# First stage: probabilities of tile pairs without zeros, weighting last, GpSimd's sum early; the mask's products in row halves

## The chip, the cores and the metric

The program runs on one core of a Trainium2 chip. The metric is the device time of one execution in microseconds (us), the smaller the better.

## The reference, cut to what matters

The program computes six residual layers over x of shape (32, 64, 256). Two of them matter here. The first is a causal attention with 16 heads of 128 over sequences of 64:

```
def _L0_attn_ref(x, W_Q, W_K, W_V, W_O, b_Q, b_K, b_V, b_O):
    q = jnp.einsum('bpd,hde->bphe', x, W_Q) + b_Q
    k = jnp.einsum('bpd,hde->bphe', x, W_K) + b_K
    v = jnp.einsum('bpd,hde->bphe', x, W_V) + b_V
    scores = jnp.einsum('bqhe,bkhe->bhqk', q, k) / ATTN_SCALE
    scores = jnp.where(causal, scores, IGNORE)
    attn = jax.nn.softmax(scores, axis=-1)
    z = jnp.einsum('bkhe,bhqk->bqhe', v, attn)
    out = jnp.einsum('bqhe,hed->bqd', z, W_O) + b_O
...
x = x + _L0_attn_ref(_layernorm(x, axis=-1), ...)
```

The others that the change touches are two causal attentions with 16 heads of 16 (one inside the third layer, one the fifth layer), whose scores get an additive mask:

```
scores = jnp.einsum('bgnqd,bgkd->bgnqk', qg, k) * scale
scores = jnp.where(causal, scores, jnp.asarray(-1e+30, scores.dtype))
attn = jax.nn.softmax(scores, axis=-1)
```

## The kernel before, in words

The 2048 tokens are 16 tiles of 128 partitions, and each tile holds two sequences of 64 tokens. x stays in on-chip memory (`x_rows`) through all stages. Products that need full accuracy are made of three products of high and low parts (`PARTS`).

**First stage** (`stage_L0_attention`). The normalised tokens are turned once (`split_tokens`) into `xnT`, with the model dimension on partitions. Then come 64 units, u = 4 x head + group of four tiles. One unit is, on TensorE (PE):

- `project` (L557): q and k of 512 tokens, six products of 512 columns each. For the even head of each pair of heads `values` (L539) makes the values of both heads, twelve products of 256 columns ahead of q and twelve behind k. So of every eight units four have values and four have none.
- `scores` (L572): eight products of 64 x 64, one for each sequence; fp32, so that each is two instructions in the trace.
- `turn` (L580): four transposes of the probabilities, 128 x 128 each. The probabilities of a tile's two sequences stand in `prob` as two 64 x 64 blocks on the diagonal of a 128 x 128 block whose other half is zeros.
- `weigh` (L589): z of each tile is one product of the turned block, 128 rows deep and 128 columns wide.
- `output` (L598): z times W_O, twelve products of 256 columns.

VectorE (DVE) does, for one unit: `shift` (L687 mask, L691 maximum, L693 subtraction), `normalise` (L717 sum, L719 reciprocal, L723 two products of 64 partitions each into `prob`), `z_low_part` (L682) and `add_out` (L701, x plus the result). ScalarE (ACT) does `q_copy` (L623), `k_copy` (L636), `v_copy` (L644), `probT_copy` (L632), `exponent` (L628) and `z_high_part` (L653), and `split_high` (L615, L618), the high parts of the next weights, once in four units.

Beside this the stage decodes the packed weights of the last layer (`Dequantiser`), one piece in four units, in phases: DVE `code` and `sign` (L2473, L2475), then `signed` (L2479), `sized` (L2484), `full` (L2490), one phase behind each unit; ACT two `over` (L2501, L2503) and later one half (L2508); GpSimd (POOL) the sum of the two `over` (`gpsimd_sum`, L2514), for which DVE's `sized` waits, and the low half (`gpsimd_low`, L2520). POOL also makes the low parts of the first stage's weights (`split_low`, L665, and L669 for the values).

The order on each engine is written out by hand: `run_steps` goes through a list of (part, lag) in every step s and gives part its unit s - lag. Each engine executes its own list in order, and semaphores tie the lists together. A part with a larger lag works on an older unit.

**The two masked attentions** (stages with tags s3a and s5a) go over 16 tiles each. Their scores are sums in PSUM: first the mask, as a product of the identity with the mask (L1283, `ident_r` 128 x 128 with `mask_r` 128 x 64 four times over, four such products of 256 columns for a tile), then the 32-row products of q and k on top of it (L1290).

## Time and profile before

| | us |
|---|---|
| median of 3 runs | 1754.83 |
| range of the runs | 1753.07 to 1756.31 |
| the profiled execution | 1752.43 |
| its span, first to last instruction | 1750.6 |

Busy shares of the span: PE 91%, DVE 62%, ACT 49%, POOL 38%. The mean granted clock of TensorE is 0.971 of full speed. The first stage's units run from 33 us (first scores) to some 559 us. A busy share is an average over stages; what bounds a stage is read from the order of instructions in it. PE's matmuls are pipelined: a group's busy time includes the tail of its last instruction, and what a group costs is read from its start to the start of the next.

### The profile page before, as it was taken

What the parts mean: (1) busy time and instruction counts of PE and PEld (TensorE: products, weight loads), DVE (VectorE), ACT (ScalarE), POOL (GpSimd) and SP (SyncE); (2) the same over time, 40 slices, a digit from 0 to 9 for tenths busy, and PEclk for the clock granted to TensorE, in tenths of its full rate; (3) what the DMA queues carried; (4) which work ended last, traced back from release to release, by engine and by line L of the source; (5) the groups of instructions that cost most, each with busy time, mean ns of one, the idle gap of its engine ahead of it and who ended that gap; (6) DMA issues with size and microseconds to landing.
All of it is one profiled execution on the core that took longest, in us unless ns stands there. A gap on an engine that the chain in (4) does not pass through costs nothing. (4 is left out here: it accounts for less than half of the span.)

```text
span 1750.6 us, 37012 instructions
## 1 busy us (share of the span) xinstructions
PE 1584.9 (91%) x14664; PEld 1281.7 (73%) x14664; DVE 1089.3 (62%) x1734; ACT 863.5 (49%) x1466; POOL 672.5 (38%) x527
## 2 busy tenths in 40 slices
PE   6999999999996887899999797899997898999998
PEld 4888888888885565777788564566664675888887
DVE  5777677677776888566442568999994565112111
ACT  3555555555453565555422346667672674222222
POOL 0111211211212663531422265999994430232332
PEclk9999999999998999899999799999998898999999
DMA  3011111111112300010102120000000900000000
GB/s 105 16 64 55 40 63 60 33 63 60 37 59 78 109 2 26 8 12 10 40 1 105 28 64 1 1 2 1 2 1 26 360 17 1 1 13 12 1 12 12
DMA packets 72351, 70.26 MB, mean 40 GB/s; under 512 B 24816, under 2 KB 64368, under 8 KB 71840
## 3 DMA queue, kind: packets, MB, share of 16 engines
q1 hardware_dynamic: 72224, 68.46, 12.2%
q8 instruction: 93, 1.52, 0.4%
q14 instruction: 34, 0.28, 0.1%
HBM read 46.03 MB, written 19.27 MB: 37 GB/s over the span
## 5 line engine op out<-in xcount | busy, mean ns | idle before, releaser
L665 POOL TENSOR_TENSOR s_w_parts<-s_w_raw,s_w_parts 128x768 fp32r<-128x768 f32 x15 | 27.8, 1855 | 401.9 <-ACT s_w_parts L615 401.9
L1488 DVE TENSOR_TENSOR s6f_hid<-s6f_act_sb,s6f_u_ps 128x512 f32<-128x512 f32 x64 | 44.0, 688 | 218.4 <-PE s6f_u_ps L1439 218.4
L1511 POOL TENSOR_TENSOR s6f_hid_parts<-s6f_hid,s6f_hid_parts 128x512 fp32r<-128x512 f32 x64 | 82.7, 1291 | 224.3 <-ACT s6f_hid_parts L1477 224.3
L2228 POOL TENSOR_TENSOR s4b_with_q<-s4b_with_q 128x1024 f32<-128x1024 f32 x64 | 150.8, 2378 | 0.4 <-DVE s4b_with_q L2183 0.4
L2183 DVE TENSOR_TENSOR s4b_with_q<-s4b_c_ps,s_q_rows 128x2048 f32<-128x2048 f32 x64 | 146.1, 2285 | 1.2 <-PE s4b_c_ps L2322 1.1
L598 PE MATMUL s_o_ps<-s_w_parts,s_zT 128*128 128x256 f32 x768 | 110.6, 294 | 4.1 <-DVE x_rows L701 4.1
L539 PE MATMUL s_v_ps<-s_wv_parts,s_xnT 128*128 128x256 f32 x768 | 104.6, 286 | 8.2 <-ACT s_v L644 6.8
L1477 ACT ACTIVATE s6f_hid_parts<-s6f_hid 128x512 fp32r<-128x512 f32 x64 | 40.5, 632 | 144.5 <-PE s6f_o_ps L1459 141.0
L539 PEld LDWEIGHTS s_v_ps<-s_wv_parts,s_xnT 128*128 128x128 f32 x768 | 97.0, 191 | 13.8 <-ACT s_v L644 10.0
L1459 PEld LDWEIGHTS s6f_o_ps<-s6w_parts,s6f_hid_parts 128*128 128x128 f32 x768 | 99.2, 188 | 6.8 <-issue 1.0
L598 PEld LDWEIGHTS s_o_ps<-s_w_parts,s_zT 128*128 128x128 f32 x768 | 97.3, 193 | 8.8 <-issue 4.5
L1439 PE MATMUL s6f_g_ps<-s_zT,s6w_parts 128*128 128x512 f32 (+1 forms) x384 | 101.2, 398 | 1.2 <-PEq L283 1.2
L557 PE MATMUL s_q_ps<-s_xnT,s_w_parts 128*128 128x512 f32 x384 | 101.7, 400 | 0.0
L1459 PE MATMUL s6f_o_ps<-s6w_parts,s6f_hid_parts 128*128 128x256 f32 x768 | 100.7, 280 | 0.8 <-POOL s6f_hid_parts L1511 0.8
L1439 PE MATMUL s6f_u_ps<-s_zT,s6w_parts 128*128 128x512 f32 (+1 forms) x384 | 100.5, 396 | 0.0
L628 ACT ACTIVATE s_ex<-s_sc 128x256 f32<-128x256 f32 x64 | 26.7, 417 | 149.2 <-DVE s_sc L693 149.2
L557 PE MATMUL s_k_ps<-s_xnT,s_w_parts 128*128 128x512 f32 x384 | 98.5, 392 | 0.0
L2306 PE MATMUL s4b_turns_ps<-s_theta_parts,s_z_parts 128*128 128x512 f32 x192 | 62.8, 435 | 26.3 <-DVE s4b_frac L2166 24.5
L1439 PEld LDWEIGHTS s6f_u_ps<-s_zT,s6w_parts 128*128 128x128 f32 x384 | 72.3, 188 | 18.0
L557 PEld LDWEIGHTS s_k_ps<-s_xnT,s_w_parts 128*128 128x128 f32 x384 | 72.1, 188 | 15.8
L1511 POOL TENSOR_TENSOR s3f_hid_parts<-s3f_hid,s3f_hid_parts 128x512 fp32r<-128x512 f32 x32 | 42.3, 1321 | 104.7 <-ACT s3f_hid_parts L1477 104.7
L701 DVE TENSOR_TENSOR x_rows<-x_rows,s_o_ps 128x1024 f32<-128x1024 f32 x64 | 77.5, 1210 | 1.6 <-PE s_o_ps L598 1.6
(333 smaller groups left out, 3982.0 us busy)
## 6 DMA issues: line engine op xcount, KB each, us to landing
stored_weights<-s1q_halves SPq DMA_DIRECT2D x16, 768.0 KB, 3.7
s6w_parts<-stored_weights SPq DMA_DIRECT2D x32, 384.0 KB, 7.6
s1q_packed<-in_codes SPq DMA_DIRECT2D x8, 384.0 KB, 4.4
s1q_scale<-in_scale_rows SPq DMA_DIRECT2D x8, 384.0 KB, 4.9
s3p_raw<-in_ffn_pieces SPq DMA_DIRECT2D x8, 384.0 KB, 8.5
early_values<-s_vbd SPq DMA_DIRECT2D x1, 2176.0 KB, 12.3
s_vbd<-early_values SPq DMA_DIRECT2D x4, 544.0 KB, 7.0
x_rows<-in_x SPq DMA_DIRECT2D x4, 512.0 KB, 5.4
```

The source lines that it names most:

```text
L539: last = nc.tensor.matmul(v_ps[:, n * 2 * E:(n + 1) * 2 * E], xnT[:, px, c, g * TG + t, :], wv_parts[:, pw, c, :, :], start=(c == 0 and (p ...
L557: last = nc.tensor.matmul(ps[:, :], weights(slot, pw, m, c), xnT[:, px, c, g * TG:(g + 1) * TG, :], start=(c == 0 and (pw, px) == PARTS[0] ...
L598: last = nc.tensor.matmul(o_ps[:, t // 2, (t % 2) * D:(t % 2 + 1) * D], zT[:, pz, t * P:(t + 1) * P], w_parts[:, k // G, pw, 2, :], start= ...
L701: nc.vector.tensor_tensor(core.x[:, t0:t0 + TG, :], core.x[:, t0:t0 + TG, :], o_ps[:, :, :].rearrange("p b (t n) -> p (b t) n", t=2), ALU. ...
L1439: last = nc.tensor.matmul(ps[:, s, :], wt(pw, c, f), zT[:, pz, c:c + 1, bass.ds(rnd * TG, TG), :] .rearrange("p c t q -> p (c t) q"), star ...
L1459: last = nc.tensor.matmul(o_ps[:, t, 0:D], hid_parts[:, f % 2, ph, t * P:(t + 1) * P], down_w(pw, f), start=(f == 0 and (ph, pw) == PARTS[0]),
L1477: nc.scalar.activation(hid_parts[:, f % 2, 0, :], hid[:, f % 2, :], ACT.Copy).then_inc(high_done, 1)
L1488: nc.vector.tensor_tensor(hid[:, f % 2, :], act_sb[:, f % 2, :], u_ps[:, f % 2, :], ALU.mult) \
L1511: nc.gpsimd.tensor_tensor(hid_parts[:, f % 2, 1, :], hid[:, f % 2, :], hid_parts[:, f % 2, 0, :], ALU.subtract).then_inc(low_done, 1)
L2183: nc.vector.tensor_tensor(with_q[:, half, :, :, :, :, :].rearrange("p (a n) q j s c -> p n a q (j s) c", n=2) [:, n_, :, :, :, :], src.uns ...
L2228: nc.gpsimd.tensor_tensor(with_q[:, half, :, 0, :, n_, :], with_q[:, half, :, 0, :, n_, :], with_q[:, half, :, 1, :, 1 - n_, :], op).then_ ...
L2306: last = nc.tensor.matmul(turns_ps[:, :], z_parts[:, pz, half, bass.ds(i * P, P)], theta_parts[:, pt, half, n_ * 512:(n_ + 1) * 512], star ...
```

## The change

**Tokens in pairs.** `split_tokens` gets `pairs=True` in the first stage: `xnT` holds two tiles 2i and 2i+1 as (first sequences of both, second sequences of both). So the 128 tokens of one `values` product are sequence b of both tiles of a pair, and the products of q and k run over the same tokens in this order.

**Probabilities without zeros.** `prob` is [P, 2, TG, S] (two buffers), written by one product over 128 partitions in place of two over 64. `turn` is two transposes for a unit in place of four: one transposes the blocks of two tiles side by side. The turned block then holds tile n's keys in rows n x 64 and queries of both sequences in its columns. `weigh` takes eight products in place of four, each 64 rows deep, 128 columns of weights, 64 columns moving, and those of n = 0 and n = 1 lie in the two halves of the rows and write to two banks of `z_ps`. `probT_copy` copies 256 columns in place of 512. `z_ps` takes two banks; to make room, `s_ps` and `pT_ps` share one bank, and with it come two waits: `scores` of u also waits for `pT_out` of u - 1 copies, and `turn` of u for `masked` up to u + 2.

**Order in the step.** PE: from project, turn, scores, output, weigh to project, turn, output, scores, weigh, with turn and weigh one unit older (lag 5) and output too (lag 6). ACT: `z_high_part` before `exponent`. DVE: `add_out` first, `z_low_part` before `normalise`. POOL: from split_low, sum, low to low, sum, split_low. The zeroing of `prob` goes.

**The mask's products.** `ident_r` holds in each half of its rows the 64 x 64 identity twice side by side, and product j reads only the row half j % 2: 64 rows deep, 256 columns as before.

```
-            prob = room.sb("prob", [P, TG, P])
-            probT = room.sb("probT", [P, TG * P])
-            zT = room.sb("zT", [P, 2, TG * P], F32R)
+            prob = room.sb("prob", [P, 2, TG, S])
+            probT = room.sb("probT", [P, TG * S])
+            zT = room.sb("zT", [P, 2, 2, 2 * P], F32R)
...
+            sp_ps = room.ps("sp_ps", [P, 512])
+            s_ps, pT_ps = sp_ps[:, 0:TG * S], sp_ps[:, TG * S:2 * TG * S]
+            z_ps = room.ps("z_ps", [P, 2, 512])
...
                     wait(pe, masked, u)
+                    wait(pe, pT_out, u - 1)
...
-                    for t in range(TG):
-                        last = nc.tensor.transpose(pT_ps[:, t * P:(t + 1) * P], prob[:, t, :], core.c("ident"))
+
+                    pe.wait_ge(masked, min(u + 2, U) if isinstance(u, int) else u + 2)
+                    for pair in range(2):
+                        last = nc.tensor.transpose(pT_ps[:, pair * P:(pair + 1) * P],
+                                                   prob[:, k % 2, 2 * pair:2 * pair + 2, :].rearrange("p t s -> p (t s)"),
+                                                   core.c("ident"))
...
-                    for t in range(TG):
-                        last = nc.tensor.matmul(z_ps[:, t * P:(t + 1) * P], v[:, k % G, t, k // G, :],
-                                                probT[:, t * P:(t + 1) * P], start=True, stop=True)
+                    for pair in range(2):
+                        for b in range(2):
+                            for n in range(2):
+                                rows, at = slice(n * S, (n + 1) * S), pair * P + b * S
+                                last = nc.tensor.matmul(z_ps[:, n, at:at + S], v[rows, k % G, pair, b, k // G, :],
+                                                        probT[rows, at:at + S], start=True, stop=True)
...
-                run_steps(pe, U, [(project, 3), (turn, 4), (scores, 3), (output, 5), (weigh, 4)], unroll=8)
+                run_steps(pe, U, [(project, 3), (turn, 5), (output, 6), (scores, 3), (weigh, 5)], unroll=8)
...
-                run_steps(act, U, [(v_copy(0), 3), (q_copy, 3), (k_copy, 3), (v_copy(1), 3), (probT_copy, 4), (exponent, 3),
-                                   (z_high_part, 4), (split_high, 0), (deq.scalar, 4)], unroll=8)
+                run_steps(act, U, [(v_copy(0), 3), (q_copy, 3), (k_copy, 3), (v_copy(1), 3), (probT_copy, 5),
+                                   (z_high_part, 5), (exponent, 3), (split_high, 0), (deq.scalar, 4)], unroll=8)
...
-                run_steps(pool, H, [(split_low, 0), (lambda j, rnd, slot: deq.gpsimd_sum(j), 1),
-                                    (lambda j, rnd, slot: deq.gpsimd_low(j, slot), 2)])
+                run_steps(pool, H, [(lambda j, rnd, slot: deq.gpsimd_low(j, slot), 2),
+                                    (lambda j, rnd, slot: deq.gpsimd_sum(j), 1), (split_low, 0)])
...
-                nc.vector.memset(prob[:, :, :], 0.0).then_inc(zeroed, 1)
-                dve.wait_ge(zeroed, 1)
...
-                    for b in range(2):
-                        rows = slice(b * S, (b + 1) * S)
-                        last = nc.vector.tensor_tensor(prob[rows, :, b * S:(b + 1) * S], ex[rows, :, :],
-                                                       rs[rows, :].unsqueeze(2).to_broadcast([S, TG, S]), ALU.mult)
-                    last.then_inc(prob_done, 1)
-
-                run_steps(dve, U, [(shift, 3), (normalise, 3), (z_low_part, 4), (add_out, 5), (deq.vector, 3)],
+                    wait(dve, pT_full, u - 1)
+                    nc.vector.tensor_tensor(prob[:, k % 2, :, :], ex[:, :, :],
+                                            rs[:, :].unsqueeze(2).to_broadcast([P, TG, S]), ALU.mult) \
+                        .then_inc(prob_done, 1)
+
+                run_steps(dve, U, [(add_out, 6), (shift, 3), (z_low_part, 5), (normalise, 3), (deq.vector, 3)],
                           unroll=8)
...
-                    nc.tensor.matmul(s_ps[:, j, 0:4 * S].rearrange("p (h s) -> p h s", s=S), ident_r[:, :],
-                                     mask_r[:, :].unsqueeze(1).to_broadcast([P, 4, S]), start=True, stop=False)
+                    half = slice(j % 2 * S, (j % 2 + 1) * S)
+                    nc.tensor.matmul(s_ps[:, j, 0:4 * S].rearrange("p (h s) -> p h s", s=S), ident_r[half, :],
+                                     mask_r[half, :].unsqueeze(1).to_broadcast([S, 4, S]), start=True, stop=False)
```

The order on PE before, in a step of a unit with values (L580 turn, L572 scores, L598 output, L589 weigh, L539 values, L557 q and k):

```order
L580 MATMUL s_pT_ps<-const,s_prob 128x128 x4
L572 MATMUL s_s_ps<-s_kT,s_qT 64x64 x8
L598 MATMUL s_o_ps<-s_w_parts,s_zT 128x256 x12
L589 MATMUL s_z_ps<-s_probT,s_v 128x128 x4
L539 MATMUL s_v_ps<-s_wv_parts,s_xnT 128x256 x12
L557 MATMUL s_q_ps<-s_xnT,s_w_parts 128x512 x6
L557 MATMUL s_k_ps<-s_xnT,s_w_parts 128x512 x6
L539 MATMUL s_v_ps<-s_wv_parts,s_xnT 128x256 x12
```

The same place on PE in the changed kernel (L589 is now turn, L612 output, L579 scores, L603 weigh):

```order
L589 MATMUL s_sp_ps<-const,s_prob 128x128 x2
L612 MATMUL s_o_ps<-s_w_parts,s_zT 128x256 x12
L579 MATMUL s_sp_ps<-s_kT,s_qT 64x64 x8
L603 MATMUL s_z_ps<-s_probT,s_v 128x64 x8
L543 MATMUL s_v_ps<-s_wv_parts,s_xnT 128x256 x12
L562 MATMUL s_q_ps<-s_xnT,s_w_parts 128x512 x6
L562 MATMUL s_k_ps<-s_xnT,s_w_parts 128x512 x6
L543 MATMUL s_v_ps<-s_wv_parts,s_xnT 128x256 x12
```

Between the last k product and the scores stood four transposes; now two transposes and the twelve output products stand there, and the scores and the weighting follow each other.

DVE before, one step of the first stage, from the mask of one unit to the decoding's phase behind it:

```order
L687 TENSOR_TENSOR s_sc<-s_s_ps,const 128x256
L691 TENSOR_REDUCE s_mx<-s_sc 128x4
L693 TENSOR_TENSOR s_sc<-s_sc,s_mx 128x256
L717 TENSOR_REDUCE s_sm<-s_ex 128x4
L719 RECIPROCAL s_rs<-s_sm 128x4
L723 TENSOR_TENSOR s_prob<-s_ex,s_rs 64x4x64 x2
L682 SCALAR_TENSOR_TENSOR s_zT<-s_z_ps,s_bias,s_zT 128x512
L701 TENSOR_TENSOR x_rows<-x_rows,s_o_ps 128x1024
L2484 TENSOR_TENSOR s1q_sized<-s1q_over,s1q_code 128x768
```

The same step on DVE in the changed kernel, with what each instruction waits for:

```order
L712 TENSOR_TENSOR x_rows<-x_rows,s_o_ps 128x1024 [waits s1_o_full]
L698 TENSOR_TENSOR s_sc<-s_sp_ps,const 128x256 [waits s1_s_full]
L702 TENSOR_REDUCE s_mx<-s_sc 128x4 [waits s1_masked]
L704 TENSOR_TENSOR s_sc<-s_sc,s_mx 128x256 [waits s1_maxed]
L693 SCALAR_TENSOR_TENSOR s_zT<-s_z_ps,s_bias,s_zT 128x512 [waits s1_z_high]
L728 TENSOR_REDUCE s_sm<-s_ex 128x4 [waits s1_exped]
L730 RECIPROCAL s_rs<-s_sm 128x4 [waits s1_summed]
L733 TENSOR_TENSOR s_prob<-s_ex,s_rs 128x256 [waits s1_pT_full,s1_inverted]
L2505 SCALAR_TENSOR_TENSOR s1q_full<-s1q_sized,s1q_signed 128x768 [waits s1q_low_done,s1q_scaled,s1q_sized_done]
```

The addition to x (L712) now stands ahead of the mask, z's low part inside the wait for the exponential, and one product of 128 partitions is left of two.

POOL before, in its loop (L665 and L669 low parts of the stage's weights, L2514 sum, L2520 low half of the decoded piece):

```order
L665 TENSOR_TENSOR s_w_parts<-s_w_raw,s_w_parts 128x768
L669 TENSOR_TENSOR s_wv_parts<-s_wv_raw,s_wv_parts 128x512
L2514 TENSOR_TENSOR s1q_over<-s1q_over 128x768
L2520 TENSOR_TENSOR s1q_halves<-s1q_full,s1q_halves 128x768
L665 TENSOR_TENSOR s_w_parts<-s_w_raw,s_w_parts 128x768
```

POOL in the changed kernel (L2535 low half, L2529 sum, L679 and L683 weights):

```order
L2535 TENSOR_TENSOR s1q_halves<-s1q_full,s1q_halves 128x768
L2529 TENSOR_TENSOR s1q_over<-s1q_over 128x768
L679 TENSOR_TENSOR s_w_parts<-s_w_raw,s_w_parts 128x768
L683 TENSOR_TENSOR s_wv_parts<-s_wv_raw,s_wv_parts 128x512
L2535 TENSOR_TENSOR s1q_halves<-s1q_full,s1q_halves 128x768
```

The sum no longer stands behind the weights of the next head, whose high parts ACT makes a step later.

## Rows read from the trace of the kernel before

**Rows 1.** First stage, 100 us: busy PE, PEld, DVE, ACT, POOL; granted clock; DMA
```profile
200.00:300.00 100.00, 95.18 (x782) 84.66 (x782) 72.36 (x127) 52.18 (x89) 18.79 (x11) 1.00 0.17 56
```

**Rows 2.** Waits of PE between 55 and 545 us: us in total, times, longest
```profile
PE s_s_ps L572 <- issue: 13.0, 31, 0.6
```

**Rows 3.** Timeline of PE: one unit without values (start us, us, instruction)
```profile
201.62 0.69 PE L572 MATMUL s_s_ps<-s_kT,s_qT 128*64 128x64 f32 x16 [0.39 <-issue]
202.23 1.69 PE L598 MATMUL s_o_ps<-s_w_parts,s_zT 128*128 128x256 f32 x12
203.76 1.05 PE L589 MATMUL s_z_ps<-s_probT,s_v 128*128 128x128 f32 x8
204.57 1.62 PE L557 MATMUL s_q_ps<-s_xnT,s_w_parts 128*128 128x512 f32 x6
206.03 1.54 PE L557 MATMUL s_k_ps<-s_xnT,s_w_parts 128*128 128x512 f32 x6
207.41 0.60 PE L580 MATMUL s_pT_ps<-const,s_prob 128*128 128x128 f32 x4
208.52 0.69 PE L572 MATMUL s_s_ps<-s_kT,s_qT 128*64 128x64 f32 x16 [0.52 <-issue]
```

**Rows 4.** Timeline of PE: units with values, the first of a round and the next
```profile
215.31 0.69 PE L572 MATMUL s_s_ps<-s_kT,s_qT 128*64 128x64 f32 x16 [0.39 <-issue]
...
223.57 1.65 PE L539 MATMUL s_v_ps<-s_wv_parts,s_xnT 128*128 128x256 f32 x12 [0.93 <-ACT s_v L644]
...
225.58 0.69 PE L572 MATMUL s_s_ps<-s_kT,s_qT 128*64 128x64 f32 x16
...
234.22 0.60 PE L580 MATMUL s_pT_ps<-const,s_prob 128*128 128x128 f32 x4
...
234.74 0.69 PE L572 MATMUL s_s_ps<-s_kT,s_qT 128*64 128x64 f32 x16
```

**Rows 5.** Timeline of ACT and DVE in the first of these units
```profile
218.17 2.58 DVE L2484 TENSOR_TENSOR s1q_sized<-s1q_over,s1q_code 128x768 f32<-128x768 f32 x1 [3.68 <-POOL s1q_over L2514]
...
222.93 0.59 ACT L644 ACTIVATE s_v<-s_v_ps 128x512 f32<-128x512 f32 x1
```

**Rows 6.** Timeline of ACT in the unit of rows 3
```profile
203.72 0.42 ACT L628 ACTIVATE s_ex<-s_sc 128x256 f32<-128x256 f32 x1 [1.71 <-DVE s_sc L693]
...
205.52 0.93 ACT L2501 ACTIVATE s1q_over<-s1q_code,const 128x768 f32<-128x768 int32 x1
...
207.17 0.67 ACT L623 ACTIVATE s_qT<-s_q_ps,s_bias 128x512 f32<-128x512 f32 x1
207.74 0.68 ACT L636 ACTIVATE s_kT<-s_k_ps,s_bias 128x512 f32<-128x512 f32 x1
```

**Rows 7.** Eight matmuls of row halves, late stage: ns min/median/max, first and last start
```profile
L2345 PE MATMUL s4b_y_ps<-s_w_bd,s4b_outT x8: 482/482/587, 1170.0 to 1171.1; 64*128 64x384 f32 x8
```

**Rows 8.** Groups of DVE between 100 and 500 us (busy us, mean ns)
```profile
L701 DVE TENSOR_TENSOR x_rows<-x_rows,s_o_ps 128x1024 f32<-128x1024 f32 x50 | 60.5, 1210 | 0.0
...
L723 DVE TENSOR_TENSOR s_prob<-s_ex,s_rs 64x256 f32<-64x256 f32 x100 | 42.0, 420 | 2.4
```

**Rows 9.** Single lines of DVE over the run: ns min/median/max, starts
```profile
L2484 DVE TENSOR_TENSOR s1q_sized<-s1q_over,s1q_code x16: 945/2566/2584, 57.6 to 542.3; 128x768 f32<-128x768 f32 x16
...
L693 DVE TENSOR_TENSOR s_sc<-s_sc,s_mx x64: 424/425/1150, 35.1 to 544.1; 128x256 f32<-128x256 f32 x64
...
L2479 DVE SCALAR_TENSOR_TENSOR s1q_signed<-s1q_sign,s1q_scale x16: 950/952/2400, 45.1 to 532.7; 128x768 f32<-128x768 int32 x16
```

**Rows 10.** Timeline of PE: the mask's products in stage s5a
```profile
1388.91 0.74 PE L1283 MATMUL s5a_s_ps<-s5a_mask_r,s5a_ident_r 128*128 128x256 f32 x4
1389.58 0.69 PE L1290 MATMUL s5a_s_ps<-s5a_kbd,s5a_qT 32*64 32x128 f32 x32
```

**Rows 11.** Waits of PE between 1370 and 1445 us (s5a)
```profile
PE s5a_va_ps L1337 <- DVE x_rows L1112: 0.6, 4, 0.2
```

**Rows 12.** Waits of POOL between 100 and 500 us
```profile
POOL s_w_parts L665 <- ACT s_w_parts L615: 316.9, 12, 28.7
```

More of the change, by code:

```diff
@@ L272, with split_tokens @@
 PARTS = ((0, 0), (0, 1), (1, 0))
-def split_tokens(core, parts, mv, factor, tag, column_step=1, beside=None, high_beside=None):
+def split_tokens(core, parts, mv, factor, tag, column_step=1, beside=None, high_beside=None, pairs=False):
     nc = core.nc
@@ L290, in rows, with place @@
         def rows(t):
+            if pairs:
+                return turned[:, t % 4, 0:D].rearrange("p (c b s) -> p c b s", c=NC, b=2)
             return turned[:, t % 4, 0:D].rearrange("p (c q) -> p c q", c=NC)
+        def place(part, t):
+            return parts[:, part, :, t // 2, :, t % 2, :] if pairs else parts[:, part, :, t, :]
         @block.vector
@@ L296, in low @@
                 dve.wait_ge(high_done, t + 1)
-                nc.vector.tensor_tensor(parts[:, 1, :, t, :], rows(t), parts[:, 0, :, t, :], ALU.subtract) \
+                nc.vector.tensor_tensor(place(1, t), rows(t), place(0, t), ALU.subtract) \
                     .then_inc(low_done, 1)
@@ L319, in _ @@
                 act.wait_ge(turned_done, t + 1)
-                nc.scalar.activation(parts[:, 0, :, t, :], rows(t), ACT.Copy).then_inc(high_done, 1)
+                nc.scalar.activation(place(0, t), rows(t), ACT.Copy).then_inc(high_done, 1)
                 if high_beside and t in (3, 9):
@@ L414, in stage_L0_attention @@
         oroom = Room(nc, octx, "s1")
-        xnT = oroom.sb("xnT", [P, 2, NC, NT, P], F32R)
+        xnT = oroom.sb("xnT", [P, 2, NC, NT // 2, 2, 2, S], F32R)
         mv = oroom.sb("mv", [P, NT, 2])
@@ L481, in low_weights @@
                                     ALU.subtract).then_inc(wv_low, 1)
-        split_tokens(core, xnT, mv, rstd, "s1t", beside=low_weights, high_beside=high_weights)
+        split_tokens(core, xnT, mv, rstd, "s1t", pairs=True, beside=low_weights, high_beside=high_weights)
         with ExitStack() as ctx:
@@ L487, in stage_L0_attention @@
             kT = room.sb("kT", [P, TG * P])
-            v = room.sb("v", [P, G, TG, 2, E])
+            v = room.sb("v", [P, G, 2, 2, 2, E])
             sc = room.sb("sc", [P, TG, S])
@@ L499, in stage_L0_attention @@
             v_ps = room.ps("v_ps", [P, 512])
-            s_ps = room.ps("s_ps", [P, 512])
-            pT_ps = room.ps("pT_ps", [P, 512])
-            z_ps = room.ps("z_ps", [P, 512])
+            sp_ps = room.ps("sp_ps", [P, 512])
+            s_ps, pT_ps = sp_ps[:, 0:TG * S], sp_ps[:, TG * S:2 * TG * S]
+            z_ps = room.ps("z_ps", [P, 2, 512])
             o_ps = room.ps("o_ps", [P, 2, 512])
             (q_full, k_full, v_full, s_full, pT_full, z_full, q_out, k_out, v_out,
-             masked, maxed, shifted, exped, summed, inverted, prob_done, pT_out, z_high, z_low, o_out, zeroed) = room.sems(
+             masked, maxed, shifted, exped, summed, inverted, prob_done, pT_out, z_high, z_low, o_out) = room.sems(
                 "q_full", "k_full", "v_full", "s_full", "pT_full", "z_full",
                 "q_out", "k_out", "v_out", "masked", "maxed", "shifted", "exped", "summed", "inverted",
-                "prob_done", "pT_out", "z_high", "z_low", "o_out", "zeroed")
+                "prob_done", "pT_out", "z_high", "z_low", "o_out")
             block = ctx.enter_context(nc.Block())
@@ L535, in values @@
                     for n in range(2):
-                        t = 2 * half + n
                         for c in range(NC):
@@ L539, in values @@
                                 last = nc.tensor.matmul(v_ps[:, n * 2 * E:(n + 1) * 2 * E],
-                                                        xnT[:, px, c, g * TG + t, :], wv_parts[:, pw, c, :, :],
+                                                        xnT[:, px, c, g * 2 + half, n, :, :].rearrange("p t s -> p (t s)"),
+                                                        wv_parts[:, pw, c, :, :],
                                                         start=(c == 0 and (px, pw) == PARTS[0]),
@@ L643, in part @@
                         act.wait_ge(v_full, u + k + half + 1)
-                        nc.scalar.activation(v[:, k, 2 * half:2 * half + 2, :, :],
-                                             v_ps[:, :].rearrange("p (t h e) -> p t h e", t=2, h=2), ACT.Copy) \
+                        nc.scalar.activation(v[:, k, half, :, :, :],
+                                             v_ps[:, :].rearrange("p (b h e) -> p b h e", b=2, h=2), ACT.Copy) \
                             .then_inc(v_out, 1)
@@ L1060, in _ @@
         def _(dve):
-            nc.vector.tensor_copy(ident_r[:, :], core.c("ident")).then_inc(masks, 1)
+            for b in range(2):
+                rows = slice(b * S, (b + 1) * S)
+                last = nc.vector.tensor_copy(ident_r[rows, :].rearrange("p (a s) -> p a s", a=2),
+                                             core.c("ident")[rows, rows].unsqueeze(1).to_broadcast([S, 2, S]))
+            last.then_inc(masks, 1)
             nc.vector.tensor_copy(mask_r[:, :], core.c("mask_add")).then_inc(masks, 1)
```

13 lines of the change are left out of this document (7 added, 6 removed).

## The prediction

> **What bounds the kernel now.** I read the views in this order: busy time by stretches, PE's waits, PE's timeline, then the timelines of the engines that PE waits for. In the first stage PE is busy 95 of 100 us at the full clock, DVE 72, ACT 52, POOL 19 [rows 1]. So PE sets the end there, and what I must count is the time from the start of one unit's scores to the start of the next. PE's waits are few by the list: the longest is 13 us in all, in front of the scores [rows 2].
>
> A unit without values takes 208.52 - 201.62 = 6.90 us [rows 3]. From start to start: scores 0.61, output 1.53, weigh 0.81, q 1.46, k 1.38, turn to scores 1.11. In the last of these the reader is to see the hidden wait: four transposes fill some 0.45 us, and the rest, about 0.65 us, is PE waiting for k's copy, which starts at 207.74 and takes 0.68 [rows 6], so it is over 0.1 us before the scores start.
>
> A unit with values takes 234.74 - 225.58 = 9.16 us; there turn to scores is only 0.52 us [rows 4], since the second half of values covers k's copy. The first such unit of each round of eight takes 225.58 - 215.31 = 10.27 us [rows 4]. Its extra 1.1 us comes in front of the second half of values, which waits for ACT's v copy at 222.93 [rows 4, 5]; and ACT is late because DVE sat idle 3.68 us for POOL's sum and then spent 2.58 us on `sized` [rows 5]. A round of eight is thus 10.27 + 3 x 9.16 + 4 x 6.8 = 65.0 us (most of the units without values take 6.8, the unit of rows 3, which has the two `over` on ACT, 6.9). There are eight rounds.
>
> **The change part by part.**
>
> *Turn.* Two transposes fewer. Four take about 0.45 us, so 0.22 us goes from each unit.
>
> *k's copy.* Output, 1.53 us, now stands between k and the scores. Turn (0.22) and output together are 1.75 us against the 1.11 us from k's end to the scores in which the copy was waited for. The copy of the turned probabilities, which the scores now also wait for, comes right behind k's copy. It has 256 columns, as the exponential has, which takes 0.42 us [rows 6]: by 1.11 + 0.4 = 1.5 us it is done, 0.25 us before PE is there. The 0.65 us of waiting goes in the four units without values; in the others nothing of it was there.
>
> *Weigh.* Eight matmuls, 16 instructions, in place of 8 instructions in 0.81 us. No row shows exactly this shape. The scores have 16 instructions of the same 64 columns, two in parallel in halves of the columns, and take 0.61 us [rows 3]. For halves of the rows there is L2345, 64 rows by 128 columns, 384 moving columns in fp32: its eight instructions start within 1.1 us [rows 7]. At the rate of weigh now (0.1 us for 128 columns) 384 columns are 0.3 us, and eight one behind another would start over 7 x 0.3 = 2.1 us. So they run two at a time. I take 0.61 us, as for the scores, which saves 0.2. The other bounds: 0.5 us if the half-deep weights come in faster; and 16 x 0.11 + 0.15 = 1.9 us if each instruction cost what one of 128 columns does now.
>
> *Change of tile form.* The four mask products of 256 columns between two other forms take 0.67 us [rows 10]; output's twelve of the same width take 1.53, 0.13 each [rows 3]. So about 0.15 to 0.2 us goes on two changes of form, and I charge 0.1 us for the one more that a unit has now (scores to weigh to q, before scores to output).
> The Trainium skill says in TensorEngine Tiling (Array Packing), Key Properties, that changing the tiling mode, not just the tile, drains TensorE. By that rule the third mode in each unit costs; without it the first stage would come out 64 x 0.1 = 6 us shorter. The trace agrees that something like 0.1 us is paid.
>
> The step of PE is then: without values 0.61 + 0.61 + 1.46 + 1.38 + 0.22 + 1.53 + 0.1 = 5.9 us; with values 9.16 - 0.22 - 0.2 + 0.1 = 8.85 us.
>
> *The chain through the scores.* What is late next when PE does not wait? The chain is scores, DVE's mask, maximum, subtraction, ACT's exponential, what ACT does behind it, q copy, k copy, probabilities' copy, next scores. From scores to the exponential it is 203.72 - 201.62 = 2.10 us [rows 6, 3]. Now `add_out`, 1.21 us [rows 8], stands ahead of the mask and starts about 0.25 us behind the scores' start, so the mask starts some 0.65 us later: 2.75. The exponential is 0.45. In one unit of four the two `over` follow, 207.17 - 205.52 = 1.65 us; then q copy 0.57 (207.17 to 207.74) [rows 6], and k copy, 0.57, and the probabilities' copy with its signal, 0.5. That is 6.5 us, over PE's 5.9. In another unit of four ACT makes high parts of weights, up to two copies of nearly the same size, and I charge the same 6.5. In the other two the chain is under 5.9. With values (8.85) it never decides. So 2 x 0.6 = 1.2 us a round.
>
> *POOL's order.* `sized` no longer waits 3.7 us. The 1.1 us in front of values goes once a round.
>
> *DVE.* It is busy 72.4% of a round of 65.0 us, 47.1 us [rows 1]; one of two products into `prob` goes, eight times 0.42 [rows 8]: 43.7 us, 5.5 a unit, under 5.9. This has little room, see the rivals. The waits for the shared bank (turn for `masked`, given a step earlier) are met more than 2 us ahead. The zeroing of `prob` is a single instruction at the stage's start, and the last units drain one step later, in which PE's work is hidden in the same chain: I take nothing for both, bounds -1 and +2 us.
>
> Round: 4 x 8.85 + 2 x 5.9 + 2 x 6.5 = 60.2 us against 65.0, 4.8 less; times eight is 38 us.
>
> *The mask's products.* Now 0.67 us for four of 256 columns [rows 10]; as two pairs that run at once I take two slots of 0.13 and the two changes of form, about 0.4 us: 0.27 us less, for 2 x 16 tiles. PE waits for next to nothing in that loop, 0.6 us in all for the worst [rows 11], so it carries: 32 x 0.27 = 8.6, and I take 8. Bounds: 0 if something else is next at once, 10 at best.
>
> Sum: 38 + 8 = 46 us. The profiled execution took 1752.43 us, 1.8 outside its span; less 46 it is 1706.4. The median of the runs is 2.4 us above it, and since the forecast is for a median I name 1708.
>
> **The rivals.**
>
> *PE decides throughout* (no chain, and weigh at 0.5). Speaks for it: the slack before and behind the chain may let late copies be caught up in the values units. Round 4 x 8.75 + 4 x 5.8 = 58.2, 6.8 less, 54 in all, with 9 for the masks: 1754.8 - 63 = 1692.
>
> *DVE becomes the bound, through POOL.* `sized` takes 945 ns at best and 2566 in the median, `signed` 952 and once 2400, the subtraction 425 and once 1150 [rows 9]: each has two tensors in on-chip memory, and in the long ones POOL was at work. Until now POOL waited once in four units, for the weights' high parts, 12 times in 400 us, and for nothing else that the list names [rows 12]: its instructions ran in one burst, part of it while DVE stood idle. Now they come in three different steps, each beside busy DVE work: `sized`, as before, `signed` (+1.45), and the product into `prob` twice a piece (up to +0.7 each by the subtraction's row, more if it comes early in POOL's instruction). That is +2.9 for four units, 5.9 a round: 49.6 us, 6.2 a unit. Over values units it is hidden, in the others it makes 6.6 to 7 of 5.9 or 6.5, since an instruction that is held makes `add_out` late and with it the chain. Round some 62.3, 2.7 less, 22 in all; with 8 of the masks 1725. Against it: most of the values units can absorb what piles up.
> The Trainium skill, GPSIMD Engine Reference, Specifications, says that GpSimd shares its SBUF interfaces with VectorE, with contention where VectorE has two SBUF inputs or a 2-port mode. The trace agrees for the two-input ones (2566 against 945 ns). By this rule `code` and `sign` could be held as well, for which no row here shows a case.
>
> *The masks give nothing* and the first stage what I say: 1716.
>
> *Slower than before: the row halves of weigh don't run together.* Its place is the group of 16 instructions behind the scores. If each costs what one of 128 columns costs now, weigh is 1.9 us, a unit without values 7.2, one with values 10.1, the round 69.2 us, 4.2 more; times eight 34, less 8: 1781. The point from which it decides: the round without weigh and without the chain is 4 x (8.24 + 5.3) = 54.2, so weigh must stay under (65.0 - 54.2 + 1) / 8 = 1.5 us (the 1 is the masks' share). Against it stands L2345's row, the same tile form.
>
> **How the numbers follow.** Chances: the forecast 0.5 (its own range 1698 to 1718), PE throughout 0.2, DVE with POOL 0.18, masks give nothing 0.08, slower 0.04. The two around the forecast on either side are taken in: the range is 1691 to 1731. A measurement of this kernel can tell about 0.2%, 3.5 us, from no change. Faster by more 0.94, within 0.02, slower 0.04.
>
> **What would show it.** In the profile after: scores to scores 5.9 us in units without values and about 8.85 in those with them; no unit of 10.3; weigh starting 0.61 us ahead of q; no idle time of DVE for POOL's sum; `prob` as one product of 0.42 us. If two units a round show 6.5, ACT or DVE in front of the scores is what I said. Long `prob` and `signed` instructions and a scores wait would show the DVE rival. In s3a and s5a the mask group should start 0.4 us ahead of the 32-row products. The forecast is wrong if weigh takes over 0.9 us, or if units without values average over 6.6 us.

## The result, and the profile after

The changed kernel takes 1734.4 us (median of 4 runs, 1731.17 to 1740.51) against 1754.62 for the kernel before (4 runs, 1753.07 to 1756.31): ratio 0.9889, 95% interval 0.9858 to 0.9919. It is faster, as forecast, but by 20 us where 46 were forecast, and the time lies outside the range of 1691 to 1731. The profiled executions differ by 1752.43 - 1731.17 = 21.3 us.

PE is busier than in [rows 1], at the same clock, and DVE less (busy by windows; the columns are those of [rows 1]):

```profile
200.00:300.00 100.00, 97.36 (x880) 87.01 (x879) 68.06 (x120) 53.35 (x93) 22.20 (x12) 1.00 0.17 56
```

The timeline of PE: first the groups of a unit without values, which answer to [rows 3], then the starts of the scores of later units, the first step without values (205.37 to 212.73), the next two with them:

```profile
190.76 0.38 PE L589 MATMUL s_sp_ps<-const,s_prob 128*128 128x128 f32 x2
190.90 1.67 PE L612 MATMUL s_o_ps<-s_w_parts,s_zT 128*128 128x256 f32 x12
192.50 0.69 PE L579 MATMUL s_sp_ps<-s_kT,s_qT 128*64 128x64 f32 x16
193.11 1.11 PE L603 MATMUL s_z_ps<-s_probT,s_v 64*128 64x64 f32 x16
194.15 1.67 PE L562 MATMUL s_q_ps<-s_xnT,s_w_parts 128*128 128x512 f32 x6
...
205.37 0.69 PE L579 MATMUL s_sp_ps<-s_kT,s_qT 128*64 128x64 f32 x16 [0.27 <-ACT s_probT L646]
...
212.73 0.69 PE L579 MATMUL s_sp_ps<-s_kT,s_qT 128*64 128x64 f32 x16 [1.01 <-ACT s_probT L646]
...
221.82 0.69 PE L579 MATMUL s_sp_ps<-s_kT,s_qT 128*64 128x64 f32 x16
...
230.83 0.69 PE L579 MATMUL s_sp_ps<-s_kT,s_qT 128*64 128x64 f32 x16
```

From start to start: turn 0.14 us, output 1.60, scores 0.61, weigh 194.15 - 193.11 = 1.04. The forecast had 0.61 for weigh, and before it was 0.81 [rows 3]. The units with values take 221.82 - 212.73 = 9.09 and 230.83 - 221.82 = 9.01 us, and that first one is no longer the 10.27 us of [rows 4]. The unit before it takes 212.73 - 205.37 = 7.36 us, with a wait of 1.01 us for ACT that was not in the forecast. Over the stage the starts of the scores are 6.27, 6.27, 6.61 and 7.2 to 8.05 us apart without values, 9.00 to 9.13 and once 9.74 with them. The six rounds of eight units in the middle of the stage take 62.4 to 63.3 us, 62.8 in the mean, against 65.0 before and 60.2 forecast.

The same unit on ACT; before, [rows 6] showed the overs and the copies without a break:

```profile
207.73 0.41 ACT L642 ACTIVATE s_ex<-s_sc 128x256 f32<-128x256 f32 x1
209.69 0.85 ACT L629 ACTIVATE s_w_parts<-s_w_raw 128x768 fp32r<-128x768 f32 x1 [1.56 <-DMA s_w_raw<-in_L_attn_W_O]
210.53 0.63 ACT L632 ACTIVATE s_wv_parts<-s_wv_raw 128x512 fp32r<-128x512 f32 x1
211.06 0.67 ACT L637 ACTIVATE s_qT<-s_q_ps,s_bias 128x512 f32<-128x512 f32 x1
211.63 0.68 ACT L650 ACTIVATE s_kT<-s_k_ps,s_bias 128x512 f32<-128x512 f32 x1
212.20 0.38 ACT L646 ACTIVATE s_probT<-s_sp_ps 128x256 f32<-128x256 f32 x1
```

ACT waits 1.56 us for the next head's weights before it makes their high part; q's, k's and the probabilities' copies are queued behind, and the scores wait for the last of them. SP's queue shows why the weights are late:

```profile
205.29 0.33 SPq L442 DMA_DIRECT2D s_bias<-in_bias_L  x1
205.89 0.38 SPq L446 DMA_DIRECT2D s_w_raw<-in_L_attn_W_Q  x1
206.37 0.42 SPq L446 DMA_DIRECT2D s_w_raw<-in_L_attn_W_K  x1
206.97 0.34 SPq L449 DMA_DIRECT2D s_w_raw<-in_L_attn_W_O  x1
```

The bias load, ahead of the weights, waits until the head two before has had its last output (its buffer is shared), and output now comes one step later.

On DVE nothing waits for POOL any more, and another instruction is held in place of `sized` (ns min/median/max of each line; [rows 9] has `sized` at 945/2566/2584 before, where `code` was 551/555/561):

```profile
L2488 DVE TENSOR_SCALAR s1q_code<-s1q_packed x16: 552/2200/2216, 38.2 to 510.0; 128x768 int32<-128x768 int32 x16
...
L2499 DVE TENSOR_TENSOR s1q_sized<-s1q_over,s1q_code x16: 943/951/953, 54.3 to 522.8; 128x768 f32<-128x768 f32 x16
```

The mask's products in stage s5a, against [rows 10]: the next group starts 0.43 us behind them instead of 0.67.

```profile
1370.58 0.50 PE L1298 MATMUL s5a_s_ps<-s5a_mask_r,s5a_ident_r 64*128 64x256 f32 x4
1371.01 0.69 PE L1305 MATMUL s5a_s_ps<-s5a_kbd,s5a_qT 32*64 32x128 f32 x32
```

The loops of s3a and s5a shrank from 103.70 to 98.58 us and from 83.19 to 79.95 us, 8.4 together. The rest came from the first stage. Its scores, first to last, took 506.97 us and take 490.37, 16.6 less. They begin 1.2 us later (34.59 us instead of 33.42), and from the last scores to the start of the last `add_out` it is 20.1 us instead of 17.8.

### The profile page after: what moved, and what is told of

Read it like the earlier page. It is cut to its first block and busy times, and to the rows that moved or that the text cites. A ratio compares the mean times of both kernels' runs of the same rounds, so it can differ in the third digit from the quotient of the medians.

```text
span 1729.4 us, 37862 instructions
## 1 busy us (share of the span) xinstructions
PE 1577.0 (91%) x15048; PEld 1270.1 (73%) x15048; DVE 1056.8 (61%) x1671; ACT 849.3 (49%) x1466; POOL 678.7 (39%) x527
## 3 DMA queue, kind: packets, MB, share of 16 engines
q8 instruction: 95, 1.56, 0.4%
## 5 line engine op out<-in xcount | busy, mean ns | idle before, releaser
L712 DVE TENSOR_TENSOR x_rows<-x_rows,s_o_ps 128x1024 f32<-128x1024 f32 x64 | 78.0, 1219 | 135.2 <-PE s_o_ps L612 135.2
L667 ACT ACTIVATE s_zT<-s_z_ps,s_bias 128x512 fp32r<-128x512 f32 x64 | 44.1, 689 | 150.0 <-PE s_z_ps L603 150.0
L612 PE MATMUL s_o_ps<-s_w_parts,s_zT 128*128 128x256 f32 x768 | 110.1, 294 | 4.6 <-DVE s_zT L693 4.6
L2535 POOL TENSOR_TENSOR s1q_halves<-s1q_full,s1q_halves 128x768 fp32r<-128x768 f32 x16 | 33.3, 2084 | 200.6 <-ACT s1q_halves L2523 200.6
L612 PEld LDWEIGHTS s_o_ps<-s_w_parts,s_zT 128*128 128x128 f32 x768 | 98.2, 194 | 5.6 <-DVE s_zT L693 5.6
```

The source lines that it names most:

```text
L612: last = nc.tensor.matmul(o_ps[:, t // 2, (t % 2) * D:(t % 2 + 1) * D], zT[:, pz, t % 2, t // 2 * P:(t // 2 + 1) * P], w_parts[:, k // G, ...
L667: nc.scalar.activation(zT[:, 0, :, :], z_ps[:, :, 0:2 * P], ACT.Identity, bias=bias[:, k // G, 2:3]) \
L712: nc.vector.tensor_tensor(core.x[:, t0:t0 + TG, :], core.x[:, t0:t0 + TG, :], o_ps[:, :, :].rearrange("p b (t n) -> p (b t) n", t=2), ALU. ...
```

## The experiments

"Before" in each ratio is the kernel before, run on the same chip. The median of each kernel and the ratio with its 95% interval:

| kernel | us | ratio to before |
|---|---|---|
| output ahead of scores, alone | 1784.28 | 1.0181 (1.0166 to 1.0195) |
| mask's row halves, alone | 1746.40 | 0.9965 (0.9952 to 0.9977) |
| GpSimd's order, alone | 1742.99 | 0.9942 (0.9929 to 0.9955) |
| all orders and halves, zeros kept | 1737.19 | 0.9912 (0.9897 to 0.9928) |
| the change | 1734.40 | 0.9889 (0.9858 to 0.9919) |
| zeros kept, loads early | 1730.18 | 0.9869 (0.9851 to 0.9887) |
| the change, loads early | 1728.25 | 0.9852 (0.9836 to 0.9869) |
| the change, weigh in quarters | 1717.42 | 0.9786 (0.9770 to 0.9802) |
| both | 1711.33 | 0.9762 (0.9745 to 0.9778) |
| both, decoder in ACT's gap | 1707.49 | 0.9745 (0.9730 to 0.9760) |
| the same, values' weights first | 1703.88 | 0.9726 (0.9709 to 0.9742) |

**Weigh in quarters.** Each product of 64 rows by 128 columns of weights becomes two of 64 by 64, behind a product of one column that carries the waits.

```
+ matmul(z_ps[0:64, 0, 256:257], v[:, ..., 0:64], probT[:, 0:1])
+ for half in range(2):  cols = slice(half * 64, half * 64 + 64)
-   matmul(z_ps[:, n, at:at+S],    v[rows, ..., :],    probT[rows, at:at+S])
+   matmul(z_ps[cols, n, at:at+S], v[rows, ..., cols], probT[rows, at:at+S])
```

> The changed kernel with weigh in quarters: the 128 columns of weights (v) are loaded as two halves of 64, so a unit has 16 products of 64 rows x 64 columns, four at a time in the quarters of the array, behind one product of one column that carries the wait. Theory A (the load of 128 columns of fp32 weights sets weigh's pace, 0.112 us for each pair, as 0.058 us goes with 64 columns in the scores): weigh takes about 0.75 us from its first product to q in place of 1.04, units without values that wait for nothing 5.95 to 6.0 in place of 6.27, with values 8.7 in place of 9.01; the units with a wait for ACT (6.6, 7.3) stay nearly as they are. About 2 us a round, 14 to 17 us in all: some 1718. Theory B (two products in row halves stream their columns one after the other, 2 x 0.056): weigh stays at 1.0 us or grows with the switch of form, and the time stays within 3 us of the changed kernel's.

Measured 1717.42 us (1715.21 to 1720.01), 17 less than the change. PE's timeline, one unit:

```profile
193.75 0.69 PE L579 MATMUL s_sp_ps<-s_kT,s_qT 128*64 128x64 f32 x16
194.27 0.23 PE L599 MATMUL s_z_ps<-s_probT,s_v 128*64 128x1 f32 x2
194.43 0.69 PE L607 MATMUL s_z_ps<-s_probT,s_v 64*64 64x64 f32 x32
195.05 1.65 PE L562 MATMUL s_q_ps<-s_xnT,s_w_parts 128*128 128x512 f32 x6
```

Thirty-two instructions take 0.62 us where sixteen took 1.04, for the same multiplications; with the product of one column, weigh is 0.78 us, and the scores ahead of it take 0.52 us instead of 0.61. Steps are 8.73 with values and 5.9 without; where ACT's chain or the late weights set the end, 6.6 to 6.96 and once 7.5.

**Half of the columns.** In the change, weigh streams 32 of each 64 columns of probabilities from the third unit on (the other half of z is not computed).

```
- probT[rows, at:at + S]
+ probT[rows, at:at + 32]
```

> The changed kernel with weigh moving only 32 of the 64 query columns of each product from the third unit on (half of z isn't computed anew). Theory A (weights' load sets the pace): the pairs of weigh still start 0.112 us apart and the group of 16 takes 1.04 us as before. Theory B (the streams of columns set it): pairs 0.06 us apart, the group about 0.6 us.

One run, 1742.71 us. The weigh group, in the timeline:

```profile
194.70 1.08 PE L604 MATMUL s_z_ps<-s_probT,s_v 64*128 64x32 f32 x16
195.71 1.66 PE L562 MATMUL s_q_ps<-s_xnT,s_w_parts 128*128 128x512 f32 x6
```

With half of the streaming it still takes 1.01 us, and its pairs still start 112 ns apart. So the moving columns don't set the pace of weigh. The weights' load is what is left, and the trace has records of it (PEld; ns min/median/max of one), here for weigh before, in the change and in quarters:

```profile
L589 PEld LDWEIGHTS s_z_ps<-s_probT,s_v x512: 186/192/331, 41.1 to 552.1; 128*128 128x128 f32 x171
...
L603 PEld LDWEIGHTS s_z_ps<-s_probT,s_v x1024: 182/188/334, 49.3 to 540.0; 64*128 64x128 f32 x171
...
L607 PEld LDWEIGHTS s_z_ps<-s_probT,s_v x2048: 129/135/223, 48.9 to 523.9; 64*64 64x64 f32 x187
```

Half of the rows leave a load as long as it was (188 ns against 192), half of the columns shorten it (135). The whole was not faster: four units with values take 10.55 to 10.59 us, each behind a unit with late weights, and the granted clock falls in them (0.54 between 152 and 154 us, in the first of them). One run doesn't tell whether that belongs to the edit.

**Weights loaded first.** The DMAs of the weights go ahead of SP's wait for the output, and the bias load, which alone needs it, behind them.

```
- wait(sp, o_full, ...);  dma(bias ...)
  wait(sp, w_low, h - 1)
  dma(w_raw ...) x3;  dma(wv_raw ...) x2
+ wait(sp, o_full, ...);  dma(bias ...)
```

> The changed kernel with one thing in the order of the loads: the DMAs of the next head's weights are issued ahead of SP's wait for the last output of the head before last, and only the bias load stays behind it. Theory: with output one step later that wait ends later, the weights land late, and ACT waits 1.6 us for them in one unit of four; in units without values this reaches the scores. Then ACT's wait for w_raw goes, that unit takes 6.3 to 6.6 in place of 7.2 to 8.0, and the time is 5 to 7 us less than the changed kernel's (about 1728), with less spread between runs. Rival: the loads are late for another reason (the DMA queue, the wait for the low parts): the unit stays at 7.3 and the time too.

Measured 1728.25 us (1724.38 to 1728.52); the profiled span is 1722.6 against 1729.4. In ACT's timeline the high parts now run on without a wait:

```profile
203.95 0.41 ACT L642 ACTIVATE s_ex<-s_sc 128x256 f32<-128x256 f32 x1
204.26 0.83 ACT L629 ACTIVATE s_w_parts<-s_w_raw 128x768 fp32r<-128x768 f32 x1
205.00 0.62 ACT L632 ACTIVATE s_wv_parts<-s_wv_raw 128x512 fp32r<-128x512 f32 x1
```

The units without values are 6.27, 6.27, 6.61 and 6.26 us in every round: the fourth was late only for its weights. The intervals of the two ratios overlap a little, so it is the profile that shows the gain: from the first scores to the last it is 481.6 us instead of 490.4.

**Both together.**

> Both edits at once. If they are independent, 20 to 23 us less than the changed kernel, about 1712. If ACT's chain (exponential, the two copies of the decoder or of the weights, q, k, probabilities) is next, units with this work stay at 6.4 to 6.6 and the sum is smaller, 1716.

Measured 1711.33 us (1710.79 to 1714.60). A round is 4 x 8.73 + 5.9 + 5.93 + 6.95 + 5.87 = 59.6 us; only the unit with the two overs is still set by ACT's chain.

**The mask alone**, in the kernel before:

> The kernel before with only the mask's products in row halves. Theory: 8 us less (1746 to 1747), since PE waits for next to nothing in the two loops: from the mask group's start to the 32-row products 0.4 us in place of 0.67, 0.27 us for each of 32 tiles. Rival: other waits of the loops take it up, and the time stays within 2 us of before.

Measured 1746.40 us; the two loops take 98.6 and 79.4 us in the profile, 8.9 less. The medians differ by 6.3 us (4.0 to 8.4 by the interval).

**GpSimd's order alone**, in the kernel before:

> The kernel before with only GpSimd's order changed (low half, sum, weights). Theory: the first unit with values of each round takes 9.1 to 9.2 us in place of 10.3, 1.1 us for eight rounds, 9 us in all: 1746. DVE's idle time for POOL's sum goes; code takes 2.2 us beside POOL and sized 0.95 in place of 2.57. Rival: what DVE is held beside POOL now comes on the path, and the time stays at 1752 to 1755.

Measured 1742.99 us, 9.7 less: the first unit with values takes 9.06 us in place of 10.28 (scores in PE's timeline):

```profile
214.93 0.69 PE L572 MATMUL s_s_ps<-s_kT,s_qT 128*64 128x64 f32 x16 [0.39 <-issue]
223.99 0.69 PE L572 MATMUL s_s_ps<-s_kT,s_qT 128*64 128x64 f32 x16
```

**Output ahead of scores alone**, in the kernel before, with no other list or lag changed:

```
- (turn, 4), (scores, 3), (output, 5), (weigh, 4)
+ (turn, 4), (output, 5), (scores, 3), (weigh, 4)
```

> The kernel before with only PE's order in the step changed: output ahead of the scores, with the lags of before and nothing else. Theory: k's copy is hidden by output, so units without values take 6.2 us in place of 6.8, with one of four held at some 6.6 by ACT's chain; 2.0 to 2.4 us a round, 16 to 19 us in all: 1736 to 1739. The units with values stay at 9.16. Rival: with output ahead of them the scores and all behind them on DVE and ACT come later, and what was waited for at the scores is waited for at turn or output: no more than 5 us.

Measured 1784.28 us, 32 us slower: neither the expected gain nor its rival came. The units without values take 7.7 us instead of 6.8. PE's waits name the cause:

```profile
PE s_o_ps L598 <- DVE x_rows L701: 38.3, 37, 1.3
```

Output waits for `add_out` of the unit before, which is last in DVE's list but for the decoder. The reordering is a loss unless `add_out` is first on DVE and everything behind turn is one lag later, as the change has it.

**The order alone.** The kernel before with all lists, lags, row halves and GpSimd's order of the change, but the probabilities with their zeros (in two buffers), four transposes, eight products in weigh and two products into `prob`.

```
- prob[P, TG, P]                     transpose(prob[:, t, :])
+ prob[P, 2, TG, P]                  transpose(prob[:, k % 2, t, :])
- PE  turn 4, scores 3, output 5, weigh 4
+ PE  turn 5, output 6, scores 3, weigh 5      (ACT and DVE as in the change)
```

> The kernel before with the change's order alone: its lists and lags on PE, ACT and DVE, GpSimd's order and the mask's row halves, while prob keeps its zeros (doubled, since it is written earlier than it is turned), with four transposes and the eight products of weigh as before. Theory: the probabilities without zeros brought PE nothing, because what two transposes less save (about 0.25 us) the slow weigh takes back (1.04 against 0.81 us) together with the third change of tile form. A unit without values is then 0.61 + 1.53 + 0.81 + 1.46 + 1.38 + 0.45 = 6.25 us, one with values 9.16; the time is that of the changed kernel within 0.5%, 1728 to 1742. Rival: the zero-free form was worth what was forecast for its turn and for DVE's one product (0.42 us a unit); then steps are 6.5 us or more everywhere and the time is 1748 or above. Second rival: DVE, with one product more, becomes the bound beside GpSimd: add_out no longer waits for output, and the steps are 6.6 to 6.9 with PE waiting for the output's or the scores' release.

Measured 1737.19 us (1734.14 to 1739.56). One unit of PE:

```profile
195.03 0.69 PE L572 MATMUL s_s_ps<-s_kT,s_qT 128*64 128x64 f32 x16
195.64 1.16 PE L589 MATMUL s_z_ps<-s_probT,s_v 128*128 128x128 f32 x8
196.56 1.63 PE L557 MATMUL s_q_ps<-s_xnT,s_w_parts 128*128 128x512 f32 x6
198.02 1.54 PE L557 MATMUL s_k_ps<-s_xnT,s_w_parts 128*128 128x512 f32 x6
199.41 0.60 PE L580 MATMUL s_pT_ps<-const,s_prob 128*128 128x128 f32 x4
199.76 1.67 PE L598 MATMUL s_o_ps<-s_w_parts,s_zT 128*128 128x256 f32 x12
201.36 0.69 PE L572 MATMUL s_s_ps<-s_kT,s_qT 128*64 128x64 f32 x16
```

Turn is 0.35 us instead of 0.14, weigh 0.92 instead of 1.04: a step of 6.33 us against 6.27 (0.45 and 0.81 were expected of turn and weigh; their sum is right). The theory holds, both rivals fall, though the units with values take 9.07 us where 9.16 were expected. Row halves and GpSimd's order alone give 0.9965 x 0.9942 = 0.9907, so with the weights late the new order of steps gives nothing on top; it does in the next kernel.

**The same with the loads first.**

> As the order-only kernel, with the weights' DMAs put ahead of the wait for the output. It is to be compared with the changed kernel with the same loads (1728.25). Theory: no unit of over 7 us for late weights; units without values 6.25 us (6.6 in the one with the two overs), with values 9.16: a round of 61.95 + 0.35 against 9.01 x 4 + 6.27 x 3 + 6.61 = 61.46, so 64/8 x 0.8 = 7 us longer at most, 1728 to 1737. Rival (the zero-free form has worth of its own): 1742 or more.

Measured 1730.18 us (1728.44 to 1731.07). Steps 9.07 and 6.33, 6.33, 6.85, 6.31. The two pairs with and without zeros differ by 0.2%, and their intervals overlap: what the zero-free form itself brought, in the shape it was given, is at most a few us. By the profiles of the pair with early loads it is 5.4 us from the first scores to the last (486.9 against 481.6).

**The decoder in ACT's gap.** On top of both edits, ACT's part of the decoder moves from the end of the list to the place between the probabilities' copy and z's, where ACT waits for weigh (the DMA and the list are else as above).

```
- (probT_copy, 5), (z_high_part, 5), (exponent, 3), (split_high, 0), (deq.scalar, 4)
+ (probT_copy, 5), (deq.scalar, 4), (z_high_part, 5), (exponent, 3), (split_high, 0)
```

> The quarter weigh and the early loads together, and ACT's part of the decoder moved from the end of its step to the place behind the probabilities' copy, where ACT waits 2.3 us for weigh. Theory: the unit of four that has the two decoder copies takes 5.9 to 6.1 us in place of 6.95 (its chain loses 1.65 us), 0.9 us a round, 7 to 8 us less than with the two edits alone (1711.3): 1704. Rival: z's high part is now late, since the decoder's copies wait for DVE's code, which is held beside POOL until close to the next step, and the gain is under 2 us or a loss.

Measured 1707.49 us (1704.58 to 1710.86), 4 us less than both together where 7 to 8 were expected, with intervals that overlap. All units without values are 5.9 us, but the first with values is 9.38 to 9.46: PE comes so early that it waits for the low part of the values' weights, which GpSimd makes behind the others.

```profile
205.19 1.68 PE L543 MATMUL s_v_ps<-s_wv_parts,s_xnT 128*128 128x256 f32 x12 [0.66 <-POOL s_wv_parts L687]
```

GpSimd's two, in its timeline:

```profile
201.10 2.08 POOL L683 TENSOR_TENSOR s_w_parts<-s_w_raw,s_w_parts 128x768 fp32r<-128x768 f32 x1 [6.75 <-ACT s_w_parts L633]
203.15 1.99 POOL L687 TENSOR_TENSOR s_wv_parts<-s_wv_raw,s_wv_parts 128x512 fp32r<-128x512 f32 x1
```

**Values' weights first.** The two splits change places, on ACT and on GpSimd.

```
- w_parts high / low;   if slot == 0: wv_parts high / low
+ if slot == 0: wv_parts high / low;   w_parts high / low
```

> The fastest version so far (weigh in quarters, weights loaded early, the decoder's two overs in ACT's gap) with the high and the low part of the values' weights made ahead of those of the other weights. Theory: in that version PE waits 0.66 to 0.8 us for wv_parts once a round, in the first unit with values; with wv_parts 2 us earlier this goes, first values unit 8.73 instead of 9.4: 8 x 0.7 = 5 us less, 1702. Rival: w_parts, now later, is waited for in its place, in front of q of the same unit, and the time stays at 1707.

Measured 1703.88 us (1700.69 to 1707.00), the fastest version here. The first unit with values, in PE's timeline, is 211.29 - 202.56 = 8.73 us, with no wait for weights:

```profile
202.56 0.69 PE L579 MATMUL s_sp_ps<-s_kT,s_qT 128*64 128x64 f32 x16
...
203.86 1.68 PE L543 MATMUL s_v_ps<-s_wv_parts,s_xnT 128*128 128x256 f32 x12
...
211.29 0.69 PE L579 MATMUL s_sp_ps<-s_kT,s_qT 128*64 128x64 f32 x16
```

The medians of the last two lie 3.6 us apart and their intervals overlap a little; the wait is gone in the profile. A round is 4 x 8.73 + 4 x 5.9 = 58.5 us.

## Why the prediction was wrong

*Weigh, the step that failed.* "I take 0.61 us, as for the scores, which saves 0.2" was wrong: it takes 1.04 and costs 0.23. The prediction had named weigh over 0.9 us as a sign that it is wrong. The pairs do run two at a time, so the rival's 1.9 us is wrong too. But in the trace pairs start 112 ns apart, and so did the products of 128 rows before, 111 to 112 ns. The scores, with 64 columns of weights, have pairs 58 ns apart, and weigh in quarters sends its four products of a place together, 58 ns behind the last four. Half of the streaming left the spacing at 112 ns, weights of half the width nearly halved the group. So each weigh was eight instructions with 128 columns of weights to load before and is eight pairs of them after, 8 x 0.112 = 0.90 us: the halved depth doesn't shorten the load, and the zeros left out of the stream don't shorten the group. The other 0.14 us lies at the two ends of the group, where the tile form changes, for which the prediction had charged 0.1 separately.

Of the two rows I leaned on, the scores [rows 3] were like weigh in the stream but not in the width of the weights. L2345 [rows 7] has weights of the same width but 384 moving columns, and its pairs start 323 ns apart, 0.84 ns a column: there the stream sets the pace. The old weigh could not tell the two apart, since at that rate its 128 moving columns stream in 108 ns, nearly what it was spaced by. A row of another attention could have (L958, 18 moving columns, two at a time; its sixteen instructions and the start of what follows):

```profile
641.07 0.65 PE L958 MATMUL s_o_ps<-s_vbd,s_probT 128*64 128x18 f32 x16
641.65 0.66 PE L942 MATMUL s_pT_ps<-const,s_ex 128*128 128x128 f32 x4
```

Its pairs start 58 ns apart, as those of the scores with 64 moving columns of the same width of weights. So it was the width of their weights that made the scores fast, and weigh's weights are twice as wide.

The Trainium skill states this in TensorE: Matmul & The Clock Gate, LDWEIGHTS (loading the stationary operand): the time goes by the number of columns loaded, P / 1.2 ns, and not by the rows. By it, as an estimate, a load of 128 columns is 107 ns and one of 64 is 53; the trace agrees, with starts 112 and 58 ns apart. I had not weighed this rule. For all units the error is 64 x 0.43 = 27 us.

*The late weights, a wait that the prediction did not have.* For the moved output it followed PE, ACT and DVE, and not SP, whose loads wait for it. The price is 8.8 us by the scores from first to last (490.4 and 481.6 us), 6.8 by the whole spans (1729.4 and 1722.6) and 6.2 by the medians.

*The ends.* Prologue and drain, taken as nothing with a bound of +2, are 1.2 + 2.3 = 3.5 us longer in the profile. The 1.2 us is not the change's: the first scores start at 34.98 and 35.19 us in the kernels with the mask or GpSimd's order alone, in which PE's work up to there is that of the kernel before, and at 33.46 in the change with early loads. The drain is in part the clock. Behind the last scores PE is idle between its groups, and the granted clock falls, in the kernel before too: 0.81 in the mean over the last 17.8 us then, 0.63 over the last 20.1 now. Output takes 2.90 us there (1.69 in [rows 3]). The kernel with zeros and early loads, whose drain has the same extra step, had a granted clock of 0.90 there and took 17.7 us. What the step costs by itself is thus not shown.

*What was right.* The masks: 8 forecast, 8.4 by the loops (alone, 6.3 by the medians). GpSimd's order: 1.1 us a round forecast, 1.2 measured. k's copy: the wait for it is gone. ACT's chain with the overs: 6.5 forecast, 6.61 measured, and 6.95 once weigh is short. In the other unit charged with 6.5 nothing was due once the weights came early (6.26), and beside a PE of 6.27 the chain costs 0.34 us a round, not 1.2. DVE stayed off the path, busy 68 of 100 us: its rival fell, though `code` is held for 1.6 us as that rival thought possible. Turn saved what was taken, 0.21 us (0.35 in the order-only kernel, 0.14 in the change). A step less its weigh was forecast at 5.29 and 8.24 us, and is 6.27 - 1.04 = 5.23 and 9.01 - 1.04 = 7.97. Of the 0.27 in the second, 0.1 is the charge for the change of form, which lies in weigh as measured, and 0.09 comes from the row that it started from: units with values take 9.07 us in some rounds before and 9.16 in others, and the forecast took 9.16.

*The balance.* For a round: 60.2 forecast, + 8 x 0.43 for weigh, - 0.9 for the chain, - 4 x (0.06 + 0.27) for the rest of the steps: 61.5 us, as measured with the loads early. The late weights add 1.3: 62.8. So each of the six middle rounds misses 2.6 us, 15 in all, and the last round, which has no weights to wait for, 1.3. The first gained nothing (its seven steps take 52.3 us, 52.1 before), which is 5 more; its steps are irregular in every kernel here, and no run shows what sets them. With the 3.5 of the ends this is the 25 us that are missing. With weigh, the loads and ACT's order mended the round is 58.5 us, under the 60.2 forecast, and the time 1703.88: the gain was there, but not in the shape of weigh that the change gave it.

## What to carry to other kernels

Before packing small products into row halves, find out what paces the ones that stand there: if it is the load of the weights, halving the rows or the stream gains nothing, and narrower weights do (here 64 instead of 128 columns, twice the instructions, 0.62 instead of 1.04 us). When a step is moved a lag later, follow the semaphore that it raises into the DMA queue too, since a load behind it in order is late although it needs nothing from it. A reordering is a set: output ahead of scores alone cost 32 us, and with the other engines' lists and lags it cost nothing, and paid once the loads were early.

## What was not expected of the hardware

- DVE's `code`, with a single input in on-chip memory, takes 2200 ns in the median beside a busy POOL and 555 ns before, where it had no such neighbour; `sized`, with two inputs, takes 951 ns now and took 2566 [rows 9]. In all 15 long ones of `code` GpSimd's low half had started 0.3 us earlier. GpSimd is held as well when DVE is first: its `wv_parts` takes 1.99 us in one of the timelines above, where a DVE instruction with two inputs runs on for 0.85 us beside it, and 1.28 in the trace of the change.
- The eight products of weigh take 0.81 us behind output [rows 3] and 0.92 us behind the scores, which have the other tile form. By the starts of single instructions the whole difference lies between the first and the second: 108 ns behind output, 213 behind the scores, and 112 for all that follow. Groups of half the width or depth lose less there: the first two pairs of scores start 107 ns apart instead of 58, those of the changed weigh 160 instead of 112.
